# Dispatch and experts of layer 0 in one block, the experts batch by batch in 32 items, rows counted by TensorE

## The reference, cut to what matters

```
cap = int(LOAD * K * max(1, T / E))                 # 256
g = einsum('btc,ce->bte', x, w_router);  gate_probs = softmax(g)
# per sequence:
top_k_probs, ei = top_k(gate_probs, 2)
flat = ei.swapaxes(0, 1).ravel();  one_hot = one_hot(flat, 16)
pos = cumsum(one_hot, axis=0) * one_hot             # which place a token has in its expert
buf = buf.at[ei2.ravel(), pos.ravel()].set(xr, mode='drop')
# per expert, over the rows of both sequences:
gg = expert_inputs @ w_gate;  h = expert_inputs @ w_fc
o = (silu(gg) * h) @ w_proj
# per sequence:
y = sum_k top_k_probs * o[ei, pos]
```

## Time and profile before

| | |
|---|---|
| median of 3 executions | 4009.0 us (4007.7 to 4018.1) |
| the profiled execution | 4002.3 us, its span 4000.7 us |
| TensorE busy | 3544.1 us, 89% of the span |
| VectorE, ScalarE, GpSimd busy | 3366.3, 2563.2, 179.9 us |
| mean granted TensorE clock | 0.937 of full speed |

### The profile page before, as it was taken

The page is one execution under the profiler, slowest core; times in us unless marked ns, Lnnn a source line. Parts: engine busy times, 40 slices in busy tenths (PEclk is TensorE's granted clock), DMA queues, the critical chain, the costliest instruction groups (busy, mean ns, idle before and its releaser), DMA issues. The chain is left out here.

```text
span 4000.7 us, 89598 instructions
## 1 busy us (share of the span) xinstructions
PE 3544.1 (89%) x30184; PEld 1592.9 (40%) x30184; DVE 3366.3 (84%) x4386; ACT 2563.2 (64%) x4698; POOL 179.9 (4%) x167
## 2 busy tenths in 40 slices
PE   6679999999999998437788799879999999999997
PEld 4323333333333334414566577623333333333332
DVE  5789999998999998502566587789999998999999
ACT  1228888887888886214222222228888887888886
POOL 0000000000000000331311000000000000000000
PEclk8869999998999999769899899969999999999998
DMA  5632111201112010134100123230101201102021
GB/s 162 169 51 99 32 25 22 36 11 33 25 22 36 11 36 9 38 118 159 49 21 21 42 68 80 61 52 15 32 19 28 36 11 33 26 21 36 11 36 48
DMA packets 134450, 184.07 MB, mean 46 GB/s; under 512 B 68313, under 2 KB 87170, under 8 KB 128908
## 3 DMA queue, kind: packets, MB, share of 16 engines
q1 hardware_dynamic: 124412, 145.31, 16.3%
q0 software_dynamic: 9648, 33.63, 2.4%
HBM read 105.90 MB, written 73.43 MB: 45 GB/s over the span
## 5 line engine op out<-in xcount | busy, mean ns | idle before, releaser
L707 DVE TENSOR_REDUCE att_l_part_max<-att_l_max_ps 128x2 f32<-128x1024 f32 x2144 | 2598.6, 1222 | 101.3 <-PE att_l_max_ps L580 99.8
L678 ACT ACTIVATE att_l_probs<-att_l_s_ps 128x512 f32<-128x512 f32 x4096 | 2225.4, 596 | 492.5 <-PE att_l_s_ps L598 243.8
L612 PE MATMUL att_l_o_ps<-att_l_probs,att_l_v_sb 128*17 128x256 f32 x16384 | 1291.5, 387 | 25.9 <-ACT att_l_o_sb L684 16.0
L598 PE MATMUL att_l_s_ps<-att_l_q_sb,att_l_k_sb 50*128 50x512 f32 x4100 | 1033.3, 499 | 12.5 <-issue 7.7
L580 PE MATMUL att_l_max_ps<-att_l_k_sb,att_l_q_sb 50*128 50x512 f32 x4288 | 898.1, 414 | 94.0 <-DMA att_l_k_sb<-k_hi 61.0
L598 PEld LDWEIGHTS att_l_s_ps<-att_l_q_sb,att_l_k_sb 50*128 50x128 f32 x4100 | 386.5, 184 | 886.6 <-ACT att_l_probs L678 873.4
L612 PEld LDWEIGHTS att_l_o_ps<-att_l_probs,att_l_v_sb 128*17 128x17 f32 x16384 | 274.1, 95 | 769.7 <-issue 405.0
L580 PEld LDWEIGHTS att_l_max_ps<-att_l_k_sb,att_l_q_sb 50*128 50x128 f32 x4288 | 419.6, 192 | 146.2 <-DVE att_l_part_max L707 79.5
L1732 DVE SCALAR_TENSOR_TENSOR ffn_acc<-ffn_qk_ps,ffn_comb,ffn_acc 128x256 f32<-128x256 f32 x256 | 123.9, 484 | 32.7 <-PE ffn_qk_ps L1643 24.3
L1240 DVE TENSOR_TENSOR moe_hid<-moe_act_gate,moe_gf_ps 128x512 f32<-128x512 f32 x16 | 11.0, 688 | 139.4 <-PE moe_gf_ps L1189 139.4
L1217 ACT ACTIVATE moe_hT<-moe_rT_ps,all_modv 128x256 f32<-128x256 f32 x64 | 30.9, 563 | 149.4 <-PE moe_rT_ps L1180 149.4
(11 more groups left out here) (214 smaller groups left out, 2357.9 us busy)
## 6 DMA issues: line engine op xcount, KB each, us to landing
att_l_k_sb<-k_hi SPq DMA_DIRECT2D x72, 256.0 KB, 8.8
att_l_q_sb<-q_hi SPq DMA_DIRECT2D x280, 64.0 KB
att_l_q_sb<-q_lo SPq DMA_DIRECT2D x140, 72.0 KB
att_l_v_sb<-v_rows SPq DMA_DIRECT2D x18, 544.0 KB, 13.6
att_l_k_sb<-k_lo SPq DMA_DIRECT2D x36, 256.0 KB, 8.8
slot_rows<-att_l_zeros POOLq DMA_DIRECT2D x8, 1024.0 KB, 13.6
moe_rows<-slot_rows SPq DMA_DIRECT2D x16, 512.0 KB
slot_out<-moe_y POOLq DMA_DIRECT2D x16, 512.0 KB
```

Source lines behind the costliest of these rows:

```text
L598: nc.tensor.matmul(s_ps[:, (j * EXPS + u * HG + h) % SB], k_sb[rows, j // GPB % 2, pair, u * P:(u + 1) * P], q_sb[rows, j % QR, pair], sta ...
L612: last = nc.tensor.matmul(o_ps[32 * h:32 * h + AUG, cols], v_sb[:, j // GPB % 2, u, h * AUG:(h + 1) * AUG], probs[:, u % 2, h, cols], star ...
L678: nc.scalar.activation(probs[:, u % 2, h], s_ps[:, (j * EXPS + u * HG + h) % SB], ACT.Exp, scale=float(HD) ** -0.5).then_inc(exp_done, 1)
L707: nc.vector.reduce_max(part_max[:, j % 2, k], max_ps[:, r], AX.X).then_inc(slot_taken, 1)
```

## The change

Both functions become one block, `finish_layer0`. The experts are worked per sequence: 32 items of 256 rows, all experts of sequence 0 first, then those of sequence 1, with a ring of 4 buffers for rows, weights and output, and two for what lies between. An item's rows, turned tiles and outputs use the PSUM of `y_ps`, `zT_ps` and `aT_ps` after the dispatch is done with them. The loops over experts are written out instead of run by the engines' loop registers. Each sequence's scatters have their own semaphore; the load of its first item's rows waits for it. SP now stores the outputs as well. The count is one accumulation in PSUM: the triangle over all 32 tiles, then for each tile s one matmul with ones whose moving operand is tile s broadcast over the tiles behind it. `count(0)` is issued ahead of `turn_normed(6)`, and `positions(0)` ahead of `normalize(7)`.

```diff
-        step, put_ready, rows_put = sem("step"), sem("put_ready"), sem("rows_put")
+        step, put_ready, rows_put = sem("step"), sem("put_ready"), [sem(f"rows_put{b}") for b in range(B)]
+        ITEMS, RING, IT = B * E0, 4, CAP // P
...
         def _(sync):
+            def load(i):
+                b, e, r = i // E0, i % E0, i % RING
+                sync.dma_start(w_gf[:, r], io.w_gate_fc[e]).then_inc(item_loaded[r], 16)
+                sync.dma_start(w_pr[:, r], io.w_proj[e]).then_inc(item_loaded[r], 16)
+                if e == 0:
+                    sync.wait_ge(rows_put[b], 16 * 2 * TPB)
+                sync.dma_start(rows[:, r], tiles(io.slot_rows)[e][:, b * IT:(b + 1) * IT]).then_inc(item_loaded[r], 16)
+
+            for i in range(RING):
+                load(i)
+            for i in range(ITEMS):
+                b, e, r = i // E0, i % E0, i % RING
+                sync.wait_ge(y_scaled, i + 1)
+                sync.dma_start(tiles(io.slot_out)[e][:, b * IT:(b + 1) * IT], y[:, r]).then_inc(item_stored[r], 16)
+                if i + RING < ITEMS:
+                    load(i + RING)
...
             def count(b):
-                hot = m.chosen[:, b].rearrange("p k t e -> p (k t e)")
-                nc.tensor.matmul(aT_ps[:, 0], m.triu_b[:], hot, start=True, stop=True)
-                nc.tensor.matmul(aT_ps[:, 1], ones[:], hot, start=True, stop=True).then_inc(counted, 1)
+                hot = m.chosen[:, b].rearrange("p k t e -> p (k t) e")
+                last = nc.tensor.matmul(aT_ps[:, 0], m.triu_b[:], hot.rearrange("p s e -> p (s e)"), start=True, stop=False, skip_group_check=True)
+                for s in range(S - 1):
+                    last = nc.tensor.matmul(upto_ps[:, s + 1:S], ones[:], hot[:, s:s + 1].broadcast_to([P, S - 1 - s, E0]),
+                                            start=False, stop=(s == S - 2), skip_group_check=True)
+                last.then_inc(counted, 1)
+
+            def turn_item(i):
+                pe.wait_ge(item_loaded[r], 48 * (i // RING + 1))
+                if i >= 2:
+                    pe.wait_ge(shift_ready, (i - 1) * KH)
+                # 4 transposes into rT_ps[:, i % 2]
+            def gate_fc(i):
+                pe.wait_ge(shift_ready, (i + 1) * KH)
+                if i >= 2:
+                    pe.wait_ge(hid_ready, i - 1)
+                # 2 x KH matmuls of 256 columns into gf_ps[:, i % 2]
+            def project_item(i):
+                pe.wait_ge(hid_ready, i + 1)
+                if i >= 2:
+                    pe.wait_ge(y_scaled, i - 1)
+                # IT matmuls of 256 columns into out_ps[:, i % 2]
...
                 project(s)
+                if s == N - 1:
+                    count(0)
                 if s >= 1:
                     turn_normed(s - 1)
...
-            count(0)
             route(N - 1)
             count(1)
+            pe.wait_ge(x_added, N * 2)
+            turn_item(0)
+            turn_item(1)
+            pe.wait_ge(h_ready, N * KH)
+            gate_fc(0)
+            pe.wait_ge(count_read, B)
+            for i in range(ITEMS):
+                if i + 2 < ITEMS:
+                    turn_item(i + 2)
+                if i + 1 < ITEMS:
+                    gate_fc(i + 1)
+                project_item(i)
...
+            shift_item(0)                      # ScalarE
+            shift_item(1)
+            silu(0)
+            for i in range(1, ITEMS):
+                if i + 1 < ITEMS:
+                    shift_item(i + 1)
+                silu(i)
...
             def positions(b):
                 hot = m.chosen[:, b].rearrange("p k t e -> p (k t) e")
                 dve.wait_ge(counted, b + 1)
-                step_done(nc.vector.memset(before[0][:, 0], 0.0),
-                          nc.vector.tensor_copy(before[0][:, 1:S], tile_ps[:, 0:S - 1]))
-                src, d = 0, 1
-                while d < S:
-                    a, c = before[src], before[1 - src]
-                    step_done(nc.vector.tensor_tensor(c[:, d:S], a[:, d:S], a[:, 0:S - d], ALU.add),
-                              nc.vector.tensor_copy(c[:, 0:d], a[:, 0:d]))
-                    src, d = 1 - src, 2 * d
-                nc.vector.tensor_tensor(place[:], upto_ps, before[src][:], ALU.add).then_inc(count_read, 1)
+                nc.vector.tensor_tensor(place[:], upto_ps, hot, ALU.mult).then_inc(count_read, 1)
...
+            hidden(0)                          # VectorE
+            for i in range(ITEMS):
+                if i + 1 < ITEMS:
+                    hidden(i + 1)
+                scale(i)
```

More of the change, by code:

```diff
@@ L876, in route_vector, with finish_layer0 @@
     assert done[0] == ROUTE_STEPS
-def finish_attention0_and_dispatch(nc, m, io):
+def finish_layer0(nc, m, io):
     with ExitStack() as ctx:
@@ L897, in finish_attention0_and_dispatch @@
         ones = sb("ones", [P, P], BF16)
-        before = [sb(f"before{i}", [P, S, E0]) for i in range(2)]
         place = sb("place", [P, S, E0])
@@ L913, in _ @@
             sync.dma_start(w_router[:], io.w_router).then_inc(loaded, 16)
+            def load(i):
[13 more added lines that the diff above has]
+                    load(i + RING)
+            for r in range(RING):
+                sync.wait_ge(item_stored[r], 16 * (ITEMS // RING))
         @block.gpsimd
@@ L968, in count @@
                     pe.wait_ge(count_read, b)
[L969 to L971 removed]
+                hot = m.chosen[:, b].rearrange("p k t e -> p (k t) e")
[5 more added lines that the diff above has]
+            def turn_item(i):
+                r = i % RING
+                pe.wait_ge(item_loaded[r], 48 * (i // RING + 1))
+                if i >= 2:
+                    pe.wait_ge(shift_ready, (i - 1) * KH)
+                for t in range(IT):
+                    for half in range(KH):
+                        last = nc.tensor.transpose(rT_ps[:, i % 2, half, t * P:(t + 1) * P], rows[:, r, t, half * P:(half + 1) * P], m.ident[:])
+                last.then_inc(turned, 1)
+            def gate_fc(i):
+                pe.wait_ge(shift_ready, (i + 1) * KH)
+                if i >= 2:
+                    pe.wait_ge(hid_ready, i - 1)
+                for v in range(2):
+                    for kh in range(KH):
+                        last = nc.tensor.matmul(gf_ps[:, i % 2, v], w_gf[:, i % RING, kh, v * HID:(v + 1) * HID], slot_hT[:, i % 2, kh],
+                                                start=(kh == 0), stop=(kh == KH - 1))
+                last.then_inc(gf_ready, 1)
+            def project_item(i):
+                pe.wait_ge(hid_ready, i + 1)
+                if i >= 2:
+                    pe.wait_ge(y_scaled, i - 1)
+                for t in range(IT):
+                    last = nc.tensor.matmul(out_ps[:, i % 2, t], hid[:, i % 2, t * P:(t + 1) * P], w_pr[:, i % RING], start=True, stop=True)
+                last.then_inc(out_ready, 1)
             pe.wait_ge(loaded, 32)
@@ L1025, in _, with shift_item, silu @@
             exponents(1)
+            def shift_item(i):
+                b = i // E0
+                act.wait_ge(turned, i + 1)
+                if i >= 2:
+                    act.wait_ge(gf_ready, i - 1)
+                for half in range(KH):
+                    nc.scalar.activation(slot_hT[:, i % 2, half], rT_ps[:, i % 2, half], ACT.Identity, bias=m.modv[:, 0, 2, half, b:b + 1],
+                                         scale=m.modv[:, 0, 3, half, b:b + 1]).then_inc(shift_ready, 1)
+            def silu(i):
+                act.wait_ge(gf_ready, i + 1)
+                if i >= 2:
+                    act.wait_ge(hid_ready, i - 1)
+                nc.scalar.activation(act_gate[:, i % 2], gf_ps[:, i % 2, 0], ACT.Silu).then_inc(silu_ready, 1)
+            shift_item(0)
[5 more added lines that the diff above has]
+                silu(i)
         @block.vector
@@ L1114, in _ @@
                 add(n)
+                if n == N - 1:
+                    positions(0)
                 normalize(n)
@@ L1119, in _ @@
                     choose(0)
-            positions(0)
             shift_logits(1)
@@ new lines, in hidden, with scale @@
+            def hidden(i):
+                dve.wait_ge(silu_ready, i + 1)
+                if i >= 2:
+                    dve.wait_ge(out_ready, i - 1)
+                nc.vector.tensor_tensor(hid[:, i % 2], act_gate[:, i % 2], gf_ps[:, i % 2, 1], ALU.mult).then_inc(hid_ready, 1)
+            def scale(i):
+                b, r = i // E0, i % RING
+                dve.wait_ge(out_ready, i + 1)
+                if i >= RING:
+                    dve.wait_ge(item_stored[r], 16 * (i // RING))
+                gate = m.gates[:, 0, 1, b].unsqueeze(1).broadcast_to([P, IT, D])
+                nc.vector.tensor_tensor(y[:, r], out_ps[:, i % 2], gate, ALU.mult).then_inc(y_scaled, 1)
```

130 lines of the change are left out of this document (17 added, 113 removed).

## The result

The changed kernel takes 3980.9 us (median of 7 runs, 3972.0 to 3988.4) against 4009.0 us in as many runs of the one before: ratio 0.993, interval 0.991 to 0.995, some 28 us less. The forecast was 3955, its range 3932 to 3992. Its profiled execution took 3980.9 us.

A forecast was written before the change was run, and what follows sets the result against it. Scatter issue, then expert loads, were taken to bound the stretch before linear attention. Last scale at 1838.0 against 1891.3 saves 53.3 us, plus 0.5 at the store: 54 less than 4009.0, so 3955 us, range 3932 to 3992.

The forecast's parts named there:

- rival (a): Expert items: loads land as late as before (L 7.1 to 9), 3974 to 4001 us; chance 0.14 beyond the forecast's own range.
- When the scatter begins: Dispatch: early count of 7.2 us puts the first scatter at 1652.6 instead of 1660.94, 8.3 us gained.
- The earlier count is free: Turning and routing wait behind count(0), but batch 1 is ready 11 us before batch 0's scatters end, so no cost.
- When the experts begin: Item 0 waits only for batch 0's 32 scatters: first transpose at 1698.1 against 1756.17.
- What an item costs: Expert items: TensorE 3.02 us each, but loads make pairs of 8.6 us, 4.3 an item.
- L: Expert items: time from issued projection of item i to first transpose of item i+4, 5.6 us (bounds 5.4 and 7.1).
- clock 1.00 after 1707: Expert items: TensorE's granted clock rises at 1706.7 and stays 1.00 through waits of 2.6 us every second item.
- rival (c): Expert items: clock falls to 0.50 and stays, 6.05 us an item on TensorE, no change, 4010 us; chance 0.06.
- One silu table load: ScalarE in the items: the table load of 1.28 us, before in each turn, is needed once in the unrolled order.
- The end: After the last scale: SP stores the last item, 0.5 us sooner, then 6 us to the linear attention as before.
- (b): Expert items: loads no bound, TensorE's 3.0 us is; 92 us saved, 3917 us; chance 0.11 including half way.
- (d): Expert items: a load takes 8.8 us like attention's loads of k, L 11.8, 31 us more, 4040 us; chance 0.07.

The follow-up runs named there:

- e5: Changed kernel with the old count (two matmuls, VectorE's doubling steps) at the new early place; one execution took 4044.8 us (kernel before 4061.5).
- e8: Changed kernel with the new 32-matmul count where the count stood before; one execution took 4062.6 us (kernel before 4061.5).
- e4: Changed kernel, but items wait for all 64 scatters of both sequences; 4017.0 us, ratio 1.0003 to the kernel before.
- e1: Changed kernel plus six useless matmuls ahead of each item's wait for loads, from item 4 on; 3966.1 us, ratio 0.987 to the kernel before.
- e2: Changed kernel with a ring of eight buffers instead of four; 3919.4 us, ratio 0.976 to the kernel before.
- e9: Changed kernel unedited, repeated as a control on a third chip; 4051.4 us, ratio 0.9993 to the kernel before.
- e11: Changed kernel with GpSimd waiting after every fourth scatter until it has landed; 4038.5 us, ratio 0.997 to the kernel before.
- e3: Changed kernel with loads issued once the replaced item's projection is done, stores on ScalarE's queue; 3951.3 us, ratio 0.983 to the kernel before.
- e12: Changed kernel with items waiting for both sequences' scatters, the edit of e4 on another chip; 4068.0 us, ratio 1.004 to the kernel before.

## Why the prediction was right, and where not

The time fell in its range, 26 us from its number: half of the expected gain did not come. The range is wider than the forecast's own, 3944 to 3976, and 3980.9 lies outside that one. It was widened to take in most of rival (a), loads that land late, and late landings are not what cost the time. So that the range held is partly luck. In its own steps:

- **When the scatter begins.** Forecast 11.0 us after the choice, measured 10.0. The count took 6.3 us and not 7.2, which was worked out for the low clock throughout; the clock was 1.00 before it ended. The prediction named one gain for place and method together; e5 and e8 part it, 7.1 to 9.4 for the place, nothing to 2.2 for the method.
- **The earlier count is free.** Right: positions of sequence 1 stand at 1677.4, 4 us ahead of the forecast, since the turning and routing behind the count ran at clock 1.00 and not at the 1.94 and 3.43 us of the low one. The scatters run on without a gap, the last at 1734.3 (forecast 1733.7). On the chips with pauses that cover is used up: there the scatters of sequence 1 start 8 us late and more, though still in time for item 16.
- **When the experts begin.** Right: 1698.6 against 1698.1. e4 shows that this step carries the whole gain.
- **What an item costs: the term that was mis-sized.** Forecast 139.2 us for the stretch, measured 166.9, 27.7 more. The changed kernel's own trace splits it: its twelve slow turns cost 20.9 us, which leaves 6.8, and those lie in the waits, 16 of them of together 40.9 us where 14 of 2.6 and 1.5 for the scatters stood (the profile leaves out some 0.2 us at each). The runs agree in the main: keeping the clock up gives 15.8 us back (e1), which is a lower bound; L was 5.9 us on average and not 5.6, some 4 us over 14 pairs; and the scatters took 7.7 us at most (e4), of which 4.2 are the clock again, where 1.5 stood. The mechanism was right: items in pairs of which one waits for the rows' load, SP's four issues ahead of it. In L, SP's part was shorter than forecast (2.4 us, not 3.0) and the landing longer (3.6, not 2.6). L lies inside the bounds of 5.4 to 7.1.
- **The clock.** The step that failed is "clock 1.00 after 1707". The prediction saw the clock hold through waits of 1.8 us, saw it low after 6 us and more, and took the side of the shorter for 2.6. It weighed only a clock that stays low, rival (c), and not one that falls at most waits and comes back, which is what happened, at less than half of (c)'s price. The prediction had cited the Trainium skill's "TensorE: Matmul & The Clock Gate", section "HAM oscillation", for (c) and set it aside because the rows of before show none of it. A wait whose length lies between two rows of different outcome should have had its price in the sum; it measured 1.4 to 3.0 us for a pair, 20.9 in all.
- **One silu table load** of 1.28 us in the items, none in the turns: right.
- **The end.** The linear attention's first load comes 3.6 us after the last scale, before 6.5: 2.9 us gained where 0.5 was forecast.
- **Rivals.** (a), loads as late as before, is not what happened, though its time of 3974 to 4001 did: the landing of 3.6 is shorter than the 4.1 of before. (b), TensorE's 3.0 us, needs eight buffers (e2). (d) did not occur.

Sum of the measured parts: the last scale ends 25.1 us earlier (1891.3 to 1866.2), the hand-over is 2.9 shorter, and this execution was 0.8 us later when the stage began: 28.8.

## What to carry to other kernels

A ring of buffers is deep enough when the items that lie between the end of a buffer's use and its next one last longer than one turnaround, from the product through store and issues to the landed load. They are fewer than the ring: the rows are turned two items ahead of their product, so of four buffers one item of 3.0 us is left, of five two, of eight five, against a turnaround of 6.0 us, which loads under full traffic lengthen by some 2. Four fell short, five nearly sufficed and eight fully did. With eight buffers the kernel was the fastest on both chips where it ran (0.976 and 0.988). A short wait of TensorE for data is to be priced twice, once as time and once as the low clock behind it, and it can be told from the duration of a matmul group of known width (1.89 against 2.80 us). To start consumers on half of the data is worth at most what the other half takes to arrive (41 us here, of which some 30 came through, all of the gain), and on some chips they lose it again to that arrival: a gain of 0.7% on one chip was not there on another.

## What the hardware showed that was not expected

- The same two kernels differ from chip to chip more than the change does: before, 4009 to 4017 us on two occasions, 4052 to 4062 on three chips; the ratio of the change is 0.993 on one and 0.9993 on another.
- On all of those three chips ScalarE and VectorE wait for 6 to 20 us while GpSimd issues indirect DMAs back to back, and the items' waits of this kind are gone where it waits after every fourth (17.2 us the longest in e9, none in e11). What blocks them isn't settled. Six such pauses in the linear attention, which no edit touches, make it 40 us longer there. No trace of the kernel before was taken on those chips, so that its 40 to 50 us more are these pauses is an inference, though a close one.
- The clock fell after waits of 1.99 us (e3), 2.08, 2.56 and 2.81 us and not after ones of 2.43, 3.01 and 3.15 us, so the length of the wait alone does not decide it. The same kernel had 10 such falls in one run (e4) and 14 in another (e12), 9.5 us apart in what they cost.
